# A Performer and per-token head attention block on one Trainium2 core: numerators turned by VectorE, head attention's operands in VectorE's order

## What is computed

```python
x = x + tanh(g_xattn) * performer(layernorm(x), ctx, ctx, random_features)
x = x + tanh(g_ffn) * ffn(layernorm(x))

# performer: 16 heads of 16 channels, 64 features, causal
q_prime = exp(q @ F) + eps;  k_prime = exp(h_k + k @ F - max(h_k)) + eps
num[t] = sum_{s<=t} (q_prime[t] . k_prime[s]) v[s];  den[t] = the same sum without v
out = num / den                       # den + 2e-6 where |den| <= 1e-6

# ffn: attention of a token's 16 heads among themselves, then 8 experts
h = rmsnorm(x);  q = h @ Wq;  k, v = split((h @ Wdown) @ Wup)
att = softmax over g of q[t, h] . k[t, g] / 4;  out[t, h] = sum_g att[h, g] v[t, g]
x = x + out @ Wo
h2 = rmsnorm(x);  gate = softmax(h2 @ Wg)
y = x + sum_e gate[e] * (h2 @ We[e])
```

## Time and profile before

| | before |
|---|---|
| time, median of 3 runs | 1117.84 us (1117.04 to 1120.37) |
| the profiled execution | 1119.66 us, span 1117.9 us |
| mean granted TensorE clock | 0.991 |
| instructions in the trace | 31579 |
| TensorE matmul records | 12867 |

### The profile page before, as it was taken

How to read it: one execution, slowest core, us unless ns; L and a number is a source line. 1 busy time by engine, 2 the same in 40 slices (tenths; PEclk the granted TensorE clock), 3 DMA queues, 4 the chain that set the end, 5 groups by cost and what they waited for, 6 DMA issues and landing times.

```text
span 1117.9 us, 31579 instructions
## 1 busy us (share of the span) xinstructions
PE 1034.7 (93%) x12867; PEld 841.2 (75%) x12867; DVE 938.5 (84%) x2173; ACT 757.0 (68%) x1563; POOL 756.8 (68%) x1111
## 2 busy tenths in 40 slices
PE   0576899999999999999999999999999999999988
PEld 0355677778888888778888787888778888888776
DVE  7578678888888988888888888888888988888886
ACT  6666767667776776777677667776776677767531
POOL 3467776677767767777777667776767777777431
PEclk9988899999999999999999999999999999999999
DMA  9410000100001001010010101000000000000000
GB/s 307 142 29 11 21 30 1 30 30 30 30 30 29 11 21 30 30 30 30 30 31 2 29 30 30 30 30 30 24 8 31 29 31 30 30 30 12 11 11 19
DMA packets 38911, 38.63 MB, mean 35 GB/s; under 512 B 3440, under 2 KB 38512, under 8 KB 38768
## 3 DMA queue, kind: packets, MB, share of 16 engines
q1 hardware_dynamic: 38384, 36.59, 10.5%
q0 software_dynamic: 384, 0.04, 0.0%
HBM read 28.23 MB, written 8.39 MB: 33 GB/s over the span
## 4 chain that ended last, share of the span: by engine, by line
PE 52%; DVE 24%; DMA 7%; ACT 7%; POOL 6%; issue 2%; SPq 1%; POOLq 0%; DVEq 0%; ACTq 0%
PE ps L1857 10%; PE ps L1858 7%; PE ps L1859 7%; DVE z L1142 6%; PE ps L1888 6%; PE ps L1903 5%; PE ps L1872 4%; DMA c_in<-in_ctx 4%; DMA x_in<-in_x 3%; PE ps L1937 3%; PE ps L1896 3%; POOL x L424 2%; POOL z L417 2%; DVE k_t L1426 2%; PE ps L1851 2%
## 5 line engine op out<-in xcount | busy, mean ns | idle before, releaser
L1142 DVE SCALAR_TENSOR_TENSOR z<-ps,gate,z 128x256 f32<-128x256 f32 x512 | 234.5, 470 | 17.4 <-PE ps L1859 8.9
L1857 PE MATMUL ps<-we_hi,h_hi 128*128 128x512 f32 (+2 forms) x640 | 238.8, 373 | 5.8 <-DVE s_sub L1296 1.7
L1858 PE MATMUL ps<-we_lo,h_hi 128*128 128x512 f32 (+2 forms) x640 | 223.7, 350 | 0.0
L1859 PE MATMUL ps<-we_hi,h_lo 128*128 128x512 f32 (+2 forms) x640 | 223.7, 349 | 0.0
L1857 PEld LDWEIGHTS ps<-we_hi,h_hi 128*128 128x128 f32 x640 | 120.2, 188 | 44.3 <-issue 18.5
L1888 PE MATMUL ps<-qf,kf 64*128 64x256 f32 x1024 | 137.4, 397 | 11.7 <-POOL qf L408 9.4
L1859 PEld LDWEIGHTS ps<-we_hi,h_lo 128*128 128x128 f32 x640 | 120.2, 188 | 17.2
L1858 PEld LDWEIGHTS ps<-we_lo,h_hi 128*128 128x128 f32 x640 | 120.5, 188 | 11.6
L1888 PEld LDWEIGHTS ps<-qf,kf 64*128 64x128 f32 x1024 | 95.1, 191 | 36.9 <-issue 19.1
L1903 PE MATMUL ps<-att,v 128*32 128x256 f32 (+1 forms) x2048 | 112.4, 339 | 1.2 <-DVE att L1218 0.9
L475 POOL TENSOR_SCALAR v_bd<-v_t,sel_blk 128x512 f32<-128x512 f32 x128 | 88.3, 710 | 13.2 <-DVE v_t L1249 13.2
(11 more groups left out here) (218 smaller groups left out, 3077.9 us busy)
## 6 DMA issues: line engine op xcount, KB each, us to landing
x_in<-in_x SPq DMA_DIRECT2D x32, 256.0 KB, 3.3
c_in<-in_ctx SPq DMA_DIRECT2D x32, 256.0 KB, 3.7
out<-z SPq DMA_DIRECT2D x32, 256.0 KB, 2.2
c_chunk<-in_ctx SPq DMA_DIRECT2D x14, 512.0 KB, 8.9
stage<-in_L_ffn_We SPq DMA_DIRECT2D x2, 1024.0 KB, 9.6
c_chunk<-in_ctx SPq DMA_DIRECT2D x2, 256.0 KB, 8.5
stage_u<-in_L_ffn_Wup SPq DMA_DIRECT2D x2, 128.0 KB, 5.7
stage_b<-in_L_ffn_bup SPq DMA_DIRECT2D x1, 256.0 KB, 6.1
```

The source lines that it names most:

```text
L1142: return dve.scalar_tensor_tensor(out=z[b % 2][:, t, :], in0=ps[:, bank, offset:offset + D], scalar=gate[:, t, ex:ex + 1], in1=z[b % 2][:, ...
L1857: pe.matmul(out, a_hi(c), b_hi(c), start=(c == 0), stop=False)
L1858: pe.matmul(out, a_hi(c), b_lo(c), start=False, stop=False)
L1859: last = pe.matmul(out, a_lo(c), b_hi(c), start=False, stop=(c == C - 1))
```

## The change

- `attend` now has a loop over its four heads (`pair`); block j of the array takes the tokens of 32-block j of each 128 (queries "(t j n)"), and all four blocks the same head. A matmul has 64 columns for the first 128 keys (2 token blocks x 32) and 32 for the second. The result is [channel, token of 32] in block j, which a transpose of 32x32 blocks turns. 32 matmuls take the place of 8 in each attend.
- `nt_t_`, `nt0_`, `nt1_` and the tiles `nt`, banks nd0 and nd1 are gone. VectorE transposes each PSUM bank (av0, av1, 128x512) straight to the SBUF tile `nd` in new steps `nd0_`, `nd1_`. `den_` reads `nd`, in one operation where there were two for each of its first two parts; `o_x_` is one operation of 512 elements.
- `q_t`, `k_t`, `v_t`, `q_bd`, `k_bd`, `v_bd` are stored with the token of 32 last, the order in which VectorE produces. The matmuls of `head_scores` and `head_mix` read `q_bd` (as weights), `k_bd` and `v_bd` (moving) with a step of 32 elements.
- All engines have new orders, banks, signals and waits. The written-out start is longer, and the loop goes from 5 to NB + 3. In TensorE's slot the features are of batch n + 2 and the last expert products of n - 2. `fq_(0)` comes ahead of the steps of the stabilizer. `load_c_` waits for `v1` of two batches before at every batch, and `v1_` for `av3` of the batch before. GpSimd's slot ends with `k_lo_`, `d_v_`; ScalarE's order from the first similarities on is `x010 x011 gexp hn x000 x001`.

The core of the diff (steps that only moved, and the lists of the order, are left out but for TensorE's slot above):

```diff
-            y00=4, y01=3, av0=2, x100=6, x101=0, x110=4, x111=7, y10=2, y11=3, av1=3, nd0=5, nd1=6, ht=3,
...
+            y00=7, y01=5, av0=6, x100=5, x101=7, x110=2, x111=3, y10=5, y11=0, av1=6, ht=2, dn=5, qq=7, kv0=6,
...
-        q_t, k_t, v_t = sb("q_t", [P, 32, H]), sb("k_t", [P, 32, H]), sb("v_t", [P, 32, HD])
-        q_bd, v_bd = sb("q_bd", [P, 32, T, H]), sb("v_bd", [P, 32, 4, HD + 1])
+        q_t, k_t, v_t = sb("q_t", [P, H, 32]), sb("k_t", [P, H, 32]), sb("v_t", [P, HD, 32])
+        q_bd, v_bd = sb("q_bd", [P, T, H, 32]), sb("v_bd", [P, 4, HD + 1, 32])
...
-        nt = sb("nt", [P, QUADS, L])
+        nd = sb("nd", [P, T, H, 32])
...
-        k_bd = sb("k_bd", [P, 32, 4, H])
+        k_bd = sb("k_bd", [P, 4, H, 32])
...
             def load_c_(b):
-                if b == 3:
+                if b >= 2:
                     sp.wait_ge(*at("v1", b - 2))
...
             def v1_(b):
-                if not b:
-                    pool.wait_ge(*at("v1_one"))
+                if b >= 1:
+                    pool.wait_ge(*at("av3", b - 1))
...
-            def nt0_(b):
-                act.wait_ge(*at("av1", b))
-                act.activation(nt[:, 0:2, :].rearrange("p a b -> p (a b)"), ps[:, BANK["av0"], :], ACT.Copy).then_inc(*up("nt0", b))
...
+            def nd0_(b):
+                if not b:
+                    dve.wait_ge(*at("av1", b))
+                dve.transpose(nd[:, :, 0:8, :], ps[:, BANK["av0"], :].rearrange("p (t h n) -> p t h n", t=T, n=32)).then_inc(*up("nd0", b))
...
+            def nd1_(b):
+                dve.wait_ge(*at("av3", b))
+                dve.transpose(nd[:, :, 8:16, :], ps[:, BANK["av1"], :].rearrange("p (t h n) -> p t h n", t=T, n=32)).then_inc(*up("nd1", b))
...
+                dve.transpose(k_t[:, :, :], qkv[:, :, D:2 * D].rearrange("p t (g d) -> p g t d", d=HD)).then_inc(*up("k_t", b))
...
             def attend(oct, half, bank):
-                for part in range(2):
-                    for j in range(4):
-                        last = pe.matmul(ps[32 * j:32 * j + 32, bank, half * L + part * P:half * L + L],
-                                         v1[:, part, 8 * oct + 2 * j + half, :],
-                                         att[:, half, j, 2 * part * P:2 * P + part * P],
-                                         start=(part == 0), stop=(part == 1), skip_group_check=True,
-                                         tile_position=(0, 32 * j))
-                return last
-
-            def numerators_turned(banks):
-                for t in range(T):
-                    for quad in range(QUADS):
-                        last = pe.transpose(
-                            ps[:, banks[t], :].rearrange("p (a j s v) -> p a s j v", a=2, s=2, v=32)[:, quad // 2, quad % 2],
-                            nt[:, quad, t * P:(t + 1) * P], ident[:, :])
+                for pair in range(4):
+                    head = 2 * pair + half
+                    for part in range(2):
+                        queries = att[:, half, pair, part * 2 * P:2 * P + part * P].rearrange("p (t j n) -> p j t n", j=4, n=32)
+                        for j in range(4):
+                            out = ps[32 * j:32 * j + 32, bank, :].rearrange("p (t h n) -> p h t n", t=T, n=32)
+                            last = pe.matmul(out[:, head, part:T], v1[:, part, 8 * oct + head, :], queries[:, j],
+                                             start=(part == 0), stop=(part == 1), skip_group_check=True,
+                                             tile_position=(0, 32 * j))
                 return last
...
-                                     q_bd[:, n, :, :].rearrange("p t h -> p (t h)"), k_bd[:, n, :, :],
+                                     q_bd[:, :, :, n].rearrange("p t h -> p (t h)"), k_bd[:, :, :, n],
...
-                                     p_t[:, 8 * a + m, :], v_bd[:, 8 * a + m, :, :].rearrange("p c d -> p (c d)"),
+                                     p_t[:, 8 * a + m, :], v_bd[:, :, :, 8 * a + m],
```

More of the change, by code:

```diff
@@ L192, in build @@
             signal("once_pe0", "most_turned stab_all"),
[L193 to L198 removed]
+            signal("pe0", "fq fkp fk Y0 X10"),
+            signal("pe1", "X01 av0 av1 av3"),
@@ L467, in yb_ @@
             @per_batch
[L468 to L478 removed]
             def q_r_(b):
+                if not b:
+                    pool.wait_ge(*at("half"))
                 pool.wait_ge(*at("q_bn", b))
@@ L608, in _ @@
+            x1_(6)
+            pq3_(7)
+            pq0_(7)
+            pk3_(7)
+            yb_(5)
+            pk1_(7)
+            pk2_(7)
+            pk0_(7)
+            g_r_(6)
+            v_bd_(5)
+            v1_(7)
+            m00_(7)
+            m01_(7)
+            q_r_(8)
+            m10_(7)
+            o_n_(5)
+            q_lo_(8)
+            m11_(7)
+            k_lo_(8)
+            d_v_(6)
+            for n in range(5, NB + 4):
                 slot(n)
@@ L1131, in _ @@
+            y_(3)
+            for n in range(5, NB + 4):
                 slot(n)
@@ L2260, in _ @@
+            pv_(4)
+            av1_(6)
+            X11_(6)
+            Y1_(6)
+            mm01_(3)
+            for n in range(5, NB + 4):
                 slot(n)
```

2517 lines of the change are left out of this document (1382 added, 1135 removed).

## The result

| | before | after |
|---|---|---|
| time, median | 1117.65 us (1117.04 to 1120.37) | 1211.34 us (1210.04 to 1212.38, 4 runs) |
| ratio, 95% interval | | 1.083 (1.082 to 1.085) |
| span of the profiled execution | 1117.9 us | 1208.3 us |
| clock granted to TensorE | 0.991 | 0.99 |
| a batch between 200 and 1000 us | 32.12 us | 35.69 us |

The change is 8% slower; the forecast was a gain of 15 us, with 1162 us as the end of its range. A batch costs 3.57 us more, taken from start to start of VectorE's step `y2_`. The start is 12.4 us shorter, the end as long as before (22 us).

The account below looks back on a forecast made before the run. TensorE bounds the kernel, idle 2.5 us in 300. -0.88 + 0.10 + 0.45 = -0.33 us a batch, x 32 = -10.5 us, with ramp and tail -5 makes -15 us: 1103 us; own range 1088 to 1114, whole range 1088 to 1162.

Parts of the forecast that it names:

- Stepped reads cost nothing: Head scores and mix: TensorE's reads with a step of 128 bytes were priced at nothing; called the weakest choice.
- The second row: VectorE's stepped read of o_tok from PSUM, 739 ns for 544 elements, taken as nearest to TensorE's stepped reads.
- twice the time: Rival, head scores and mix: stepped reads double their time, +1.85 us a batch, +59 us, 1162 us; rival's chance 0.20.
- The two cycles a column: Head scores: 56 ns for 64 columns, two cycles of 2.4 GHz a column, so the reader may keep up.
- VectorE net nothing: VectorE: two PSUM transposes +1.40 us, saved 1.14 and about 0.2; 4 us of idle time a batch as cover.
- new waits: Rival: av0's mask late behind ScalarE's copies; 0.8 us a batch gives +26 us, 1129 us; chance 0.06.
- The cut attend: Value matmuls cut in four: an attend 0.69 us for 0.67, four of them 0.1 us more a batch.
- the line through the wider ones: Step time as columns / 1.2 plus some 3 ns, from 64, 68 and 256 columns; gives 30 ns at 32.
- floor at 56 ns: Rival, attends: 32-column steps stay at 56 ns, +0.83 us a batch, +27 us, 1130 us; chance 0.12.
- Turn -0.88: TensorE: the eight transposes of the numerators go, saving 0.79 + 0.09 = 0.88 us a batch.
- changes of shape +0.45: TensorE: 14 changes of array form a slot instead of 11, 2.58 us for 2.13, +0.45 us a batch.
- Ramp and tail -5 us: Start and end of the kernel: work found earlier saves 5 us in all; bounds 0 and 20.

Follow-up runs that it names:

- section 3: Three runs of the kernel before with head attention's operands stored in token groups, reads stepping 8, 16 or 32 bytes: 1115.5, 1158.7 and 1216.7 us.
- e15: Changed kernel with head attention's operands in pairs of tokens (step of 8 bytes) and the subtraction h_lo_ moved behind h2_lo1_: 1138.1 us, ratio 1.015.
- e12: Kernel before with the new attend and VectorE's transposes of the numerators, the first placed ahead of the next batch's normalisation statistics: 1217.6 us, ratio 1.090.
- e10: Kernel before with the scores' moving operand in groups of eight tokens (32 bytes) and the mix's in groups of four (16 bytes): 1216.7 us.
- e3: Changed kernel with q_bd alone stored as before, so the scores read weights without steps and k_bd with steps: 1203.8 us.
- e1: Changed kernel with q_bd, k_bd and v_bd stored as before, so ScalarE and GpSimd write with steps, TensorE reads without: 1211.9 us, ratio 1.084.

## Why the prediction was wrong

- *Stepped reads cost nothing: wrong, and the step that failed first.* "The second row is the nearer, and I take nothing", on the strength of a stepped read from PSUM by VectorE. What TensorE showed is 2.9 times the time in the scores and 2.0 in the mix, 2.65 us a batch, where twice the time, on which the upper end of my range stood, gave 1.85. The two cycles a column, which I took for slack in which a reader keeps up, did not cover it. The rule of the Trainium skill that stood against the choice ("SBUF — State Buffer", the note on cachelines, two hits in a line) holds, by the runs of section 3.
- *VectorE net nothing, "it stays at 261 of 300 us": wrong, the second failure.* It is busy 30.4 us a batch (255.61 / 300 x 35.69), 2.4 more than before, of which the rows named here make 1.6. The transposes were right (+1.42 and -1.13 us). `o_x` got hardly shorter (916 ns for two of 479), the denominators cost 0.26 us more, h2e 0.65 and the two var_f steps 0.40; of these three the slow rows end with an instruction of GpSimd. And I treated VectorE as an amount, with 4 us of slack as cover, and not as a chain: the turn of the second product, denominators, `o_x`, biases and the turn of the keys stand in a row between av3 and the bank of the key features. That wait is 1.3 us a batch. The rival "new waits" had the price (0.8 us) near, and the wrong place (the mask of av0).
- *The cut attend: half right.* A step of 32 columns takes about 30 ns (28 to one, 32 to the next), as the line through the wider ones gave; there is no floor at 56 ns, and the rival with it falls. What the runs refute is that price. "About 60 cycles" in the Trainium skill, "TensorEngine Tiling (Array Packing)", section "Instruction Overhead", are 25 ns at 2.4 GHz, an estimate from its figure, and such a floor could not show in steps of 30. (The lower bound of 29 ns, called the streaming alone, is 27 by the same line: columns / 1.2.) An attend takes 0.72 us, then 0.82 to 0.84, so four cost 0.2 us more, not 0.1. What I never priced is the code: 184 records more a batch (192 in the attends, less the eight transposes), and stops for it of 0.4 us a batch in the changed kernel, 0.9 in e15, 1.7 in e12. It is hidden while the stepped stages run slowly, and appears as soon as they are mended.
- *Turn -0.88, changes of shape +0.45, attend +0.10, in all -0.33 us: about right.* The batch of the changed kernel is 3.57 us longer. Stepped stages 2.65, waits 1.29 + 0.36 - 0.26 = 1.39 leave -0.47 for the rest. In e15 it is 1.05 us longer; waits 1.55 - 0.26 and 0.1 for the pairs leave -0.34. The parts weren't measured singly.
- *Ramp and tail -5 us:* -12.4 and +0.3. Right in sign, inside its bounds.

Why the 71 us of the layout and the rest don't add: in the changed kernel a batch is a loop over all engines, and a wait that appears in it can also cost clock. Restoring the layout alone gave 24 us, pairs 47, pairs and one moved step 73. What stays, 20 us in e15, is about the waits: 1.55 us a batch against 0.26, some 40 us, less the ramp's 12 and TensorE's own -0.3 us a batch.

## What to carry to other kernels

Before a layout is changed to spare one engine, look at the step in bytes with which every other engine then reads or writes it: 8 bytes were nearly free for TensorE's reads (0.04 to 0.07 us a stage) and VectorE's writes here, 16 bytes doubled a stage of matmuls. Price moved work as a link of a chain, not as a share of an engine's idle time, and ask which port its operands now use. Cutting matmuls into shorter ones costs code as well as columns: count how many instructions a run of short stages uses in the time that the next piece takes to come. And look at the granted clock of a batch before its times are taken for a price: in the batch shown above the matmul behind the scores takes 0.25 us more than in the median batch, by the clock alone.

## What the hardware showed that I had not expected

- TensorE's code comes in pieces of 16 KB, 126 matmuls with their weights. Runs of 192 matmul records in 2.5 us outran it by up to 2.0 us, and the stops ended 1.2 to 1.6 us after a landing. Traffic of loads made the longest 1 us longer (2.9 against 1.8).
- The step of 8 bytes is nearly free, that of 16 bytes is not, in moving operands (0.94, 1.00 and 1.97 us in the mix); 32 bytes in the scores cost less than 128 (1.89 us in e10, 2.8 in e3, the weights unstepped in both).
- At 1.2 GHz the stepped scores of the changed kernel take 2.48 to 2.68 us, as at 2.4 GHz (2.49 to 2.68), while unstepped ones take 1.87 for 1.03 (e1).
- Operations of VectorE of 32 columns, 180 to 220 ns by themselves, last until GpSimd's instruction ends, 1.19 us in the row shown and 1.32 at the most, when their operands are in SBUF. One that read PSUM took 168 ns beside GpSimd's work on `z`.
- Steps also lengthen the writes of ScalarE (708 ns; 743 at a step of 8 bytes, 1206 at 32 bytes, 1159 at 256) and GpSimd (710; 1253 at 16 bytes, 1235 at 32, 1224 at 272).
